# Two value products put side by side in the first two cycles of a batch, in a fused attention and expert kernel

## What is computed

```python
xn = layernorm(x)
# attention on xn (a second layernorm with weights goes first), 16 heads of 16, rotary q and k
scores = einsum('bhqd,bhkd->bhqk', q, k) / sqrt(16)
attn = softmax(scores, axis=-1)
out = einsum('bhqk,bhkd->bhqd', attn, v)
attn_out = xn + out @ Wo.T + bo
# experts on xn: 8 experts, each takes its 256 top rows of a batch
h = silu(x_sel @ Wg) * (x_sel @ Wu);  contrib = (h @ Wd) * gating
x_out = x + attn_out + scatter_add(contrib)
```

## Time and profile before

| what | value |
|---|---|
| times of three executions | 1746.42, 1746.68, 1751.88 us |
| median | 1746.68 us |
| profiled execution, its time | 1744.11 us |
| profiled execution, its span | 1742.3 us |
| TensorE, share of the span | 97% |
| ScalarE, share of the span | 69% |
| VectorE, share of the span | 59% |
| GpSimd, share of the span | 29% |

### The profile page before, as it was taken

How to read it: one execution, slowest core, us unless ns; L and a number is a source line. 1 busy time by engine, 2 the same in 40 slices (tenths; PEclk the granted TensorE clock), 3 DMA queues, 4 the chain that set the end, 5 groups by cost and what they waited for, 6 DMA issues and landing times.

```text
span 1742.3 us, 28948 instructions
## 1 busy us (share of the span) xinstructions
PE 1693.1 (97%) x11240; PEld 971.8 (56%) x11240; DVE 1031.3 (59%) x2053; ACT 1198.2 (69%) x1419; POOL 511.3 (29%) x479
## 2 busy tenths in 40 slices
PE   6799999999999999999999999999999999999997
PEld 4234344344444434434434433368888888888886
DVE  8664476476457466558547648856455555454543
ACT  5688988888888898898898899963333333343322
POOL 3121121101201111112112100036656565656563
PEclk9899999999999999999999999999999999999998
DMA  4644654764666458456475465445444443535332
GB/s 154 160 110 111 143 106 110 162 121 110 153 128 137 118 130 167 107 131 145 116 157 98 111 147 125 66 143 107 100 91 64 91 89 67 97 61 95 64 56 30
DMA packets 113842, 195.03 MB, mean 112 GB/s; under 512 B 20880, under 2 KB 59664, under 8 KB 113680
## 3 DMA queue, kind: packets, MB, share of 16 engines
q1 hardware_dynamic: 83552, 141.96, 37.0%
q0 software_dynamic: 29040, 49.83, 15.0%
q10 hardware_dynamic: 1088, 1.05, 0.2%
HBM read 116.22 MB, written 76.55 MB: 111 GB/s over the span
## 4 chain that ended last, share of the span: by engine, by line
PE 90%; DVE 4%; DMA 2%; issue 1%; ACT 1%; POOL 1%; SPq 1%; DVEq 0%; ACTq 0%
PE o_ps L993 26%; PE score L1072 20%; PE score L979 19%; PE side L862 5%; PE score L1084 5%; PE o_ps L1084 3%; PE side L872 3%; PE side L1084 2%; PE side L903 2%; PE side L846 2%; PE score L1059 1%; DVE stats L1121 1%; DMA o_sums<-o_sb 1%; DMA probs<-in_wo_t 0%; PE side L853 0%
## 5 line engine op out<-in xcount | busy, mean ns | idle before, releaser
L767 ACT ACTIVATE probs<-score 128x1024 f32<-128x1024 f32 x1024 | 974.3, 1048 | 121.9 <-PE score L979 121.9
L993 PE MATMUL o_ps<-probs,v_ones 128*32 128x512 f32 x4096 | 504.4, 601 | 5.1 <-DVE o_sb L1436 4.8
L979 PE MATMUL score<-q_stack,k_stack 50*128 50x512 f32 x2048 | 407.7, 462 | 5.8 <-issue 3.3
L979 PEld LDWEIGHTS score<-q_stack,k_stack 50*128 50x128 f32 x2048 | 166.2, 185 | 349.6 <-ACT probs L767 295.0
L751 ACT ACTIVATE probs<-score 128x512 f32<-128x512 f32 x128 | 76.6, 598 | 334.3 <-PE score L1072 334.3
L677 POOL DMA_INDIRECT out<-probs,rot x128 | 204.3, 1596 | 212.8 <-DVE probs L1399 183.5
L993 PEld LDWEIGHTS o_ps<-probs,v_ones 128*32 128x32 f32 x4096 | 101.6, 108 | 221.6 <-issue 146.7
L1384 DVE TENSOR_TENSOR probs<-score,probs 128x512 f32<-128x512 f32 x128 | 88.5, 691 | 206.6 <-PE score L1072 179.8
L655 POOL TENSOR_TENSOR square<-qk 128x512 bf16<-128x512 f32 x56 | 77.2, 1407 | 400.1 <-DVE qk L1241 400.1
L1072 PE MATMUL score<-parts,q_stack 128*128 128x512 f32 x640 | 158.3, 390 | 0.0
L666 POOL DMA_INDIRECT qk<-xn_rows,rot x128 | 134.2, 1048 | 38.5 <-issue 29.3
(11 more groups left out here) (273 smaller groups left out, 2559.2 us busy)
## 6 DMA issues: line engine op xcount, KB each, us to landing
q_parts<-parts SPq DMA_DIRECT2D x16, 1024.0 KB, 4.4
k_parts<-parts SPq DMA_DIRECT2D x16, 1024.0 KB, 7.3
q_stack<-q_parts SPq DMA_DIRECT2D x62, 256.0 KB, 7.3
k_stack<-k_parts SPq DMA_DIRECT2D x62, 256.0 KB, 9.4
q_stack<-q_parts SPq DMA_DIRECT2D x66, 128.0 KB, 8.1
k_stack<-k_parts SPq DMA_DIRECT2D x66, 128.0 KB, 8.8
o_sums<-o_sb SPq DMA_DIRECT2D x256, 32.0 KB
num<-o_sums SPq DMA_DIRECT2D x32, 256.0 KB
```

The source lines that it names most:

```text
L767: act.activation(probs[probs_of(b, s)][:, 2 * i:2 * i + 2, :], score[ring_of(b, p)][:, :, :], ACT.Exp, scale=SCALE).then_inc(exp_done, 1)
L979: last = pe.matmul(score[ring_of(b, p)][:, w, :], k_stack[par][rows, i, kt * P:(kt + 1) * P], q_stack[par][rows, i, qh * HALF:(qh + 1) * H ...
L993: last = pe.matmul(o_ps[j * KEYS_W:(j + 1) * KEYS_W, :], v_ones[par][:, kt, j, :], probs[probs_of(b, s)][:, j, :], start=kt == 0, stop=kt ...
```

## The change

It gives the cycles 0 and 1 of the batches 1 to 6 the paired order. In cycle 0, V(62) and V(63) of the batch before now both stand ahead of S(1); in cycle 1, V(0) and V(1) both stand ahead of S(3). Batch 0 and batch 7 (no batch before, or none after) and cycle 31 keep the parted order. No instruction is added or taken away, on any engine.

```diff
                 scores(b, 2 * c)
+                parted = c not in jobs.by_cycle and (nxt is None or prev is None or c > 1)
                 weigh_past(b, 2 * c - 2, prev)
-                if c in jobs.by_cycle:
+                if not parted:
                     weigh_past(b, 2 * c - 1, prev)
                 scores(b, 2 * c + 1)
-                if c not in jobs.by_cycle:
+                if parted:
                     weigh_past(b, 2 * c - 1, prev)
```

## The result

| | before | after |
|---|---|---|
| median of 22 executions | 1748.69 us | 1752.57 us |
| lowest to highest | 1745.64 to 1753.67 us | 1749.96 to 1755.37 us |
| ratio after to before | | 1.0018, 95% interval 1.001 to 1.0026 |
| span of the profiled execution | 1742.3 us | 1749.8 us |

The change makes the kernel slower, by 0.18% or 3.1 us, with an interval of 1.7 to 4.5 us; the two medians differ by 3.9 us. This is less than a single measurement can tell from no change, and clear only over 22 executions. The page hardly shows it: TensorE's busy time is the same as before, and the idle time of ScalarE in front of its exponentials has grown from 121.9 us to 128.7.

What follows compares the result with a forecast made beforehand. The prediction took ScalarE to bound the batch starts, TensorE the projection cycles. Losses of 0.60 + 0.38 + 4 x 0.65 = 3.6 us on a median of 1746.7 gave 1750.3 us, range 1746.5 to 1755.5.

Steps and rivals of the forecast that it cites:

- ScalarE bounds the start of a batch: At a batch start without a job, ScalarE ends last: busy 9.26 of 9.30 us, TensorE 8.40.
- V(63) ahead of S(1) costs 0.3 us, which the next step hides: Cycle 0: E(2) at 751.09 instead of 750.8, 0.3 us of ScalarE lost, hidden by the move in cycle 1.
- V(1) ahead of S(3): 0.88 us at E(6), 0.65 at E(10): Cycle 1: E(6) 0.88 us late; cycle 2 then takes 3.96 us, leaving E(10) 0.65 us late.
- The copy stays: VectorE's copy of the old sums, behind norm2, stays at 752.50 in batch 5 although V(63) ends earlier.
- Batch 1: 0.60 us: Start of batch 1, where the copy did wait for V(63): E(10) at 201.64 against 201.04, 0.60 us later.
- Batch 2: 0.38 us: Start of batch 2, E(10) already unusually late: 0.38 us, or 0.65 if that lateness has its own cause and repeats.
- Nothing gives it back: After the starts, the delay lasts to the end; the rival that it is given back, 1746.7 us, had chance 0.12.
- Fewer switches making it faster: Rival: TensorE bounds the twelve paired cycles, which save 0.34 us each, 4.1 us in all, 1742.6 us; chance 0.03.
- Cycle 2 keeping its 4.19 us: Rival at the batch starts: the 0.88 us stays whole at E(10), 5.2 us in all, 1751.9 us; chance 0.15.
- The clock: Rival: waits at batch starts let TensorE's clock fall, 1.7 to 3.4 us a batch, 1760 to 1770 us; chance 0.04.

Runs made afterwards that it cites:

- e1: The kernel before with only cycle 0 of batches 1 to 6 given the paired order, cycle 1 left parted; ratio 1.0012 to the kernel before.
- e2: The kernel before with only cycle 1 of batches 1 to 6 given the paired order, cycle 0 left parted; ratio 1.0021 to the kernel before.
- e3: The kernel before, with VectorE copying the last batch's sums inside norm2 in batches 1 to 6; ratio 0.998 to the kernel before.
- e4: The changed kernel, with VectorE copying the last batch's sums inside norm2 in batches 1 to 6; ratio 1.0007 to the kernel before.
- e8: The kernel before with the parted order also in cycles whose job is light (x, z, logits, square, peak); ratio 0.9945 to the kernel before.
- e6: The changed kernel, with batch 7's eight loads of group 2's stacks issued before the wait for the reciprocals' store; ratio 1.0067 to the kernel before.

## Why the prediction was right

**ScalarE bounds the start of a batch.** Right. TensorE's busy time in that stretch fell by 0.37 us and the stretch grew longer.

**V(63) ahead of S(1) costs 0.3 us, which the next step hides.** Right in kind, and e1 shows it covered, 0.0 us in four batches. E(2) lands where it was forecast, 5.84 us after E(-4) (forecast 5.85), but the loss is 0.40 us and not 0.3: before, E(2) stood at 5.44. The text had put it at 6 x 0.92, and 0.92 is the run of ten divided by ten, with the full length of the last one in it; the starts are 0.91 us apart on average.

**V(1) ahead of S(3): 0.88 us at E(6), 0.65 at E(10).** Right in both sizes. E(6) stands 10.43 us after E(-4) in batch 5, before 9.56: 0.87; E(10) 0.64. e2 has the same with cycle 1 alone.

**The copy stays.** Right, to the hundredth: 7.26 us after E(-4) in both.

**Batch 1: 0.60 us.** Right: 13.78 us from E(-4) to E(10) against 13.19.

**Batch 2: 0.38 us.** This is the term that was mis-sized; it measured 0.65. The text had allowed for it: the lateness of 0.67 us at E(10) has a cause of its own. In every kernel that keeps cycle 2 paired, E(10) of batch 2 comes about 0.27 us later than elsewhere (idle 0.46 us where the other batches have 0.19, in e3 and e4 too); in the kernel after it starts 0.88 us behind the start of its scores, in batch 5 0.60. What delays it stays open. With 0.65 in its place the sum is 3.85 us, and the table has 3.75.

**Nothing gives it back.** Right: the distance to the next batch grew by 0.6 to 0.7 us in each of the six but batch 3, where it grew by 1.7 with the fall of the clock.

**The rivals.** Fewer switches making it faster: the saving on TensorE is real and worthless here. The rule of the Trainium skill behind it (TensorEngine Tiling (Array Packing), Tiling Modes, Key Properties, that a change of tiling mode drains TensorE) has the sign that the rows show, 0.12 us for a pair, and e8 goes the other way: more switches, and 9 us faster. Cycle 2 keeping its 4.19 us: it took 3.96.

**The clock.** The prediction gave this rival 0.04, with 10 to 20 us if it came in all six starts, and named a clock under 1.00 in those stretches as a sign of being wrong. That sign appeared once: the clock fell to 0.50 in batch 3 of the profiled execution, and cost 1.1 us, less than the 1.7 to 3.4 that were put on it. In the other five starts it was 1.00. It doesn't carry the result, as e6 has all six starts at 1.00 and the full 3.75 us. But TensorE's idle time in a start grew, from 0.90 to 0.72 + 0.55 us in batch 5, and how often the clock falls there isn't known.

In time the forecast was 3.6 us over the kernel before; the ratio gives 3.1, the medians 3.9. The 1750.3 us was counted from a median of three executions, which lies 2 us under that of 22, and the measured median is 1752.57. That the profiles differ by 7.5 us and not 3.6 is nothing the prediction has; half of it is the clock in batch 3 and cycle 31 of batch 7.

## What to carry to other kernels

When two engines pass work to each other through a short ring, an order is judged by the holes it makes in the engine that is full in that stretch, not by what it saves on the engine that is busiest overall: two products side by side save TensorE a little and put 1.86 us instead of 0.99 between two score steps. With this ring of three pairs that leaves holes of 0.19 to 0.23 us; a deeper ring might cover them, which was not tried. Here alternating was worth 9 us in the cycles with a light job; the heavy projection cycles were left paired and were not tried. A piece that is late for another reason (the copy behind norm2) both hides small losses ahead of it and is itself worth 3.5 us to move; before a load is moved ahead of another in one queue, look for who waits for the one that is passed.

## What the runs showed that was not expected

A stack load in batch 7 took 16.50 us to land in e1, whose program issues the same transfers as the kernel before, in which TensorE did not wait for it at all. Moving these loads ahead by some five microseconds made the transfer that they passed take 16.89 us, and the kernel 8.7 us slower. The clock fell to 0.50 in two starts of a batch behind waits that each were under 0.9 us, and stayed at 1.00 behind the same waits elsewhere. And E(6) 0.87 us late left 0.64 us, two holes of 0.2 left the same, and where the next cycle had no hole of its own all of 0.85 stayed: the price of one and the same edit was 0.64 or 0.85 us a batch, by what stood around it, and that of its half in cycle 0 was nothing.
